# Two heads' scores and row maxima on one TensorE: the second head one product behind the first, and all eight PSUM banks in one ring

## What is computed

```python
q = (x @ Wq + bq).reshape(b, lq, H, D)
k = (embeds @ Wk + bk).reshape(b, lk, H, D)
v = (embeds @ Wv + bv).reshape(b, lk, H, D)
scores = jnp.einsum('bqhd,bkhd->bhqk', q, k) * SCALE
attn = jax.nn.softmax(scores, axis=-1)
ctx = jnp.einsum('bhqk,bkhd->bqhd', attn, v).reshape(b, lq, AD)
return ctx @ Wo + bo
```

## Time and profile before

| | us |
|---|---|
| median of three runs | 3068.25 |
| lowest and highest | 3066.65, 3070.2 |
| the profiled execution | 3069.01 |
| its span | 3067.2 |

### The profile page before, as it was taken

The page is one execution under the profiler, slowest core; times in us unless marked ns, Lnnn a source line. Parts: engine busy times, 40 slices in busy tenths (PEclk is TensorE's granted clock), DMA queues, the critical chain, the costliest instruction groups (busy, mean ns, idle before and its releaser), DMA issues.

```text
span 3067.2 us, 83608 instructions
## 1 busy us (share of the span) xinstructions
PE 2833.7 (92%) x28504; PEld 2329.2 (76%) x28504; DVE 2158.0 (70%) x4113; ACT 1687.2 (55%) x3422; POOL 2128.3 (69%) x1708
## 2 busy tenths in 40 slices
PE   5799999999999999999999999999999999998371
PEld 3688887888888888888888888888788888886241
DVE  6777777777777777777777777777777777774104
ACT  2466665656656656656566566566565665663020
POOL 2377777777777777777777777777777777776305
PEclk9799999999999999999999999999999999998586
DMA  3100000000000000000000000000000000000022
GB/s 97 40 1 12 2 13 3 13 2 12 3 2 13 2 13 2 13 3 13 2 13 3 2 13 2 13 2 13 3 13 2 14 14 2 2 1 1 21 92 62
DMA packets 65446, 42.02 MB, mean 14 GB/s; under 512 B 6614, under 2 KB 62635, under 8 KB 65010
## 3 DMA queue, kind: packets, MB, share of 16 engines
q1 hardware_dynamic: 62962, 32.35, 3.7%
q0 software_dynamic: 2048, 3.91, 0.5%
HBM read 28.15 MB, written 8.39 MB: 12 GB/s over the span
## 4 chain that ended last, share of the span: by engine, by line
PE 89%; issue 5%; POOL 3%; DVE 1%; ACT 0%; DMA 0%; POOLq 0%; DVEq 0%; ACTq 0%
PE ps L1315 28%; PE ps L1329 23%; PE ps L1289 8%; PE ps L1278 4%; PE ps L1279 3%; PE ps L1280 3%; PE ps L1262 3%; PE ps L1263 3%; PE ps L1264 3%; PE ps L1338 2%; PE ps L1347 2%; PE ps L1269 2%; PE ps L1437 1%; PE ps L1444 1%; PE ps L1297 1%
## 5 line engine op out<-in xcount | busy, mean ns | idle before, releaser
L587 POOL TENSOR_TENSOR key_sums<-key_sums,prob_T 128x512 f32<-128x512 f32 (+1 forms) x1408 | 1811.7, 1287 | 120.8 <-ACT prob_T L749 3.8
L977 DVE TENSOR_REDUCE mx<-ps 128x1 f32<-128x400 f32 (+1 forms) x2048 | 1077.0, 569 | 507.7 <-PE ps L1289 467.2
L749 ACT ACTIVATE prob_T<-ps 128x512 f32<-128x512 f32 x1536 | 834.1, 596 | 232.0 <-PE ps L1315 214.0
L1329 PE MATMUL ps<-prob_T,v_sb 128*64 128x256 f32 (+1 forms) x6656 | 742.4, 380 | 0.9 <-ACT prob_T L752 0.9
L1329 PEld LDWEIGHTS ps<-prob_T,v_sb 128*64 128x64 f32 (+1 forms) x6656 | 479.7, 137 | 242.1 <-issue 3.6
L583 POOL TENSOR_TENSOR key_sums<-prob_T 128x512 f32<-128x512 f32 x128 | 164.8, 1288 | 564.2 <-PE ps L1315 451.8
L1315 PE MATMUL ps<-shift,shift_w 64*128 64x256 f32 (+1 forms) x3328 | 509.5, 300 | 0.1
L1315 PE MATMUL ps<-q_hi,k_hi 64*128 64x256 f32 (+1 forms) x3328 | 476.6, 280 | 0.0
L1315 PE MATMUL ps<-q_lo,k_hi 64*128 64x256 f32 (+1 forms) x3328 | 475.1, 279 | 0.0
L1315 PE MATMUL ps<-q_hi,k_lo 64*128 64x256 f32 (+1 forms) x3328 | 473.7, 278 | 0.0
L738 ACT COPY heads_raw<-ps 128x256 f32<-128x256 f32 x128 | 47.7, 372 | 672.9 <-PE ps L1329 672.9
(11 more groups left out here) (173 smaller groups left out, 3600.0 us busy)
## 6 DMA issues: line engine op xcount, KB each, us to landing
ctx_raw<-in_ctx_dram SPq DMA_DIRECT2D x16, 768.0 KB
tables<-in_L_ffn_W_dram SPq DMA_DIRECT2D x16, 256.0 KB, 3.7
slots_in<-zeros SPq DMA_DIRECT2D x32, 64.0 KB
xs<-in_x_dram SPq DMA_DIRECT2D x8, 256.0 KB, 3.1
xres<-in_x_dram SPq DMA_DIRECT2D x8, 256.0 KB, 2.9
v_sb<-slots_in SPq DMA_DIRECT2D x8, 256.0 KB, 2.7
slots_out<-v_sb SPq DMA_DIRECT2D x8, 256.0 KB, 4.0
out_dram<-x1s SPq DMA_DIRECT2D x8, 256.0 KB, 2.4
```

Source lines behind the costliest of these rows:

```text
L587: op = nc.gpsimd.tensor_tensor(acc[0:rows, :, :], acc[0:rows, :, :], prob_T[0:rows, :, k, :], ALU.add)
L749: nc.scalar.activation(prob_T[:, h, 2 * i:2 * i + 2, :].rearrange("p k t -> p (k t)"), ps[:, bank, :], ACT.Exp).then_inc(ring_act, 1)
L977: v.tensor_reduce(mx[:, qt, h, c:c + 1], ps[:, at.bank("mx", r, c, qt, h), 0:WID[c]], AX.X, ALU.max).then_inc(ring_dve, 1)
L1329: last = mm(ps[h * DH:h * DH + DH, HEADS, 0:T], v_sb[0:rows, r % NJ // 2 % 2, k, v0 + h * DH:v0 + h * DH + DH], prob_T[0:rows, h, k, :], s ...
```

## The change

Three things are changed together.

1. The ring has all eight banks, and the result of `attend` is a place in it ("pv", the last of a slot). Its own semaphores go; `attend` waits for the bank of its place and for the last exponential.
2. A unit is issued in another order. Head 1's score products stand one step behind head 0's, and the two products of the maxima fill the holes: A0, M1, A1, B0, A2, B1, ... A7, B6, M0, B7. Each of the four banks is waited for on its own. The list of places has the order A, M1, B, M0, so with eight banks each of the four needs the bank that the same kind of product had in unit `i` - 2. The wait for B's bank stands ahead of A1, since `bank_of` for it is called right behind A0 and M1.
3. `ring_full` is no longer counted by scores and maxima: head 0's and head 1's have a counter each, `rows_full[h]`.

VectorE reduces head 1's maxima before head 0's in each pair. No product, exponential, reduction or copy is added or taken away.

```diff
-RING = (0, 1, 2, 3, 4, 5, 6)
-HEADS = 7
+RING = (0, 1, 2, 3, 4, 5, 6, 7)
...
         for i, unit in enumerate(MAX_UNITS):
+            if i < UNITS:
+                put("act", "s", s, i, 0)
             if following:
-                maximum(s + 1, unit)
+                maximum(s + 1, unit, 1)
             if i < UNITS:
-                for h in range(2):
-                    put("act", "s", s, i, h)
+                put("act", "s", s, i, 1)
+            if following:
+                maximum(s + 1, unit, 0)
...
+        put("act", "pv", s)
...
-                copy(heads_raw[:, :], ps[:, HEADS, 0:T]).then_inc(heads_free, 1)
+                act.wait_ge(ring_full, at.full("pv", r))
+                copy(heads_raw[:, :], ps[:, at.place_of("pv", r), 0:T]).then_inc(ring_act, 1)
...
-            def maximum(at, r, c, qt):
+            def maximum(at, r, c, qt, h):
                 pe.wait_ge(kh_ok, at.n(4, r, c + 1))
                 pe.wait_ge(qh_ok, at.n(1, r, 1))
-                banks = banks_of(at, *[("mx", r, c, qt, h) for h in range(2)])
...
+            def score_unit(at, s, i, unit):
+
                 tiles = [k for k in (2 * i, 2 * i + 1) if k < KT]
...
+                steps = [(n, k, step) for n, k in enumerate(tiles) for step in range(4)]
+
+                first, = banks_of(at, ("s", s, i, 0), also=[("k", s, 3), ("q", s), ("sh", s)] if i == 0 else [])
+                for at_step, part in enumerate(steps):
+                    ahead = score_step(s, 0, first, *part)
+                    if at_step == 0:
+                        if unit:
+                            maximum(at, s + 1, *unit, 1)
+                        second = bank_of(at, "s", s, i, 1)
+                    else:
+                        score_step(s, 1, second, *steps[at_step - 1])
+                ahead.then_inc(rows_full[0], 1)
+                if unit:
+                    maximum(at, s + 1, *unit, 0)
+                score_step(s, 1, second, *steps[-1]).then_inc(rows_full[1], 1)
...
             def attend(at, r):
-                wait(pe, heads_free, at.n(1, r, 0))
-
-                _, count = at.freed("s", r, UNITS - 1, 1)
-                pe.wait_ge(ring_act, count)
+
+                bank, = banks_of(at, ("pv", r), also=[("s", r, UNITS - 1, 1)])
```

More of the change, by code:

```diff
@@ L53, with maker @@
 UNITS = 7
+MAKERS = ("rows0", "rows1", "all")
+def maker(key):
+    return f"rows{key[-1]}" if key[0] in ("s", "mx") else "all"
 def value_fills(s):
@@ L65, in batch_fills, with maximum @@
     put = lambda owner, *key: fills.append((key, owner))
-    def maximum(r, unit):
-        for h in range(2):
-            put("dve", "mx", r, *unit, h)
+    def maximum(r, unit, h):
+        put("dve", "mx", r, *unit, h)
     if kind == "start":
@@ L79, in batch_fills @@
         for unit in MAX_UNITS:
-            maximum(0, unit)
+            maximum(0, unit, 1)
+            maximum(0, unit, 0)
         for c in range(4):
@@ L123, in owned @@
 def owned(kind, upto=None):
-    owners = [o for _, o in FILLS[kind][:upto]]
-    return {"full": len(owners), "act": owners.count("act"), "dve": owners.count("dve")}
+    fills = FILLS[kind][:upto]
+    owners, makers = [o for _, o in fills], [maker(key) for key, _ in fills]
+    return {"act": owners.count("act"), "dve": owners.count("dve"), **{m: makers.count(m) for m in MAKERS}}
 def bank_at(kind, place):
@@ L138, in __init__ @@
         self.start = {}
-        for of in ("full", "act", "dve"):
+        for of in ("act", "dve", *MAKERS):
             n_start, n_first, n_mid = (owned(k)[of] for k in ("start", "first", "mid"))
@@ L170, in full @@
     def full(self, *key):
-        return self._count("full", *self.find(*key))
+        return self._count(maker(key), *self.find(*key))
     def freed(self, *key):
@@ L179, in bank, with place_of @@
         return bank_at(self.kind, PLACE[self.kind][key])
+    def place_of(self, *key):
+        own, place = self.find(*key)
+        return bank_at(self._kind(own), place)
     def held_by(self, *key):
@@ L402, in decoder_layer @@
         ring_full = sem("ring_full")
+        rows_full = [sem(f"rows_full{h}") for h in range(2)]
         ring_act = sem("ring_act")
@@ L717, in values_out @@
                 if n == 0 and at.kind != "start":
-                    wait(act, pv_ok, at.n(1, 2 * g - 3, 1))
+                    if at.kind != "first" or g > 1:
+                        act.wait_ge(ring_full, at.full("pv", 2 * g - 3))
                 src = ps[:, at.bank("v", g, n), :].rearrange("p (k n) -> p k n", n=2 * P)
@@ L974, in maxima @@
                 for c, qt in units:
-                    for h in range(2):
-                        dve.wait_ge(ring_full, at.full("mx", r, c, qt, h))
+                    for h in (1, 0):
+                        dve.wait_ge(rows_full[h], at.full("mx", r, c, qt, h))
                         v.tensor_reduce(mx[:, qt, h, c:c + 1], ps[:, at.bank("mx", r, c, qt, h), 0:WID[c]],
@@ L1298, in row_shift @@
                 last.then_inc(ring_full, 1)
-            def score_unit(at, s, i):
-                banks = banks_of(at, *[("s", s, i, h) for h in range(2)],
-                                 also=[("k", s, 3), ("q", s), ("sh", s)] if i == 0 else [])
-                tiles = [k for k in (2 * i, 2 * i + 1) if k < KT]
-                rows = P if i < UNITS - 1 else KREM
-                for n, k in enumerate(tiles):
-                    cols = slice(k * P, k * P + rows)
-                    for step in range(4):
-                        for h in range(2):
-                            lanes = slice(h * DH, h * DH + DH)
-                            keys_part = (shift_w[lanes, 0:rows], k_hi[s % 2][lanes, cols], k_hi[s % 2][lanes, cols],
-                                         k_lo[s % 2][lanes, cols])[step]
-                            query_part = (shift, q_hi[s % 2], q_lo[s % 2], q_hi[s % 2])[step]
-                            last = mm(ps[0:rows, banks[h], n * T:n * T + T], keys_part, query_part[lanes, :],
-                                      start=(step == 0), stop=(step == 3))
-                            if step == 3 and k == tiles[-1]:
-                                last.then_inc(ring_full, 1)
@@ new lines, in score_step @@
+            def score_step(s, h, bank, n, k, step):
+                rows = P if k < KT - 1 else KREM
+                lanes, cols = slice(h * DH, h * DH + DH), slice(k * P, k * P + rows)
+                keys_part = (shift_w[lanes, 0:rows], k_hi[s % 2][lanes, cols], k_hi[s % 2][lanes, cols],
+                             k_lo[s % 2][lanes, cols])[step]
+                query_part = (shift, q_hi[s % 2], q_lo[s % 2], q_hi[s % 2])[step]
+                return mm(ps[0:rows, bank, n * T:n * T + T], keys_part, query_part[lanes, :],
+                          start=(step == 0), stop=(step == 3))
@@ L1390, in _ @@
             for unit in MAX_UNITS:
-                maximum(at, 0, *unit)
+                maximum(at, 0, *unit, 1)
+                maximum(at, 0, *unit, 0)
             for c in range(4):
```

33 lines of the change are left out of this document (15 added, 18 removed).

## The result

| | kernel before | changed kernel |
|---|---|---|
| median, same chip (7 runs each) | 3067.44 us | 3055.71 us |
| lowest and highest | 3064.69, 3070.2 | 3054.17, 3060.12 |
| the profiled execution | 3069.01 | 3059.33 |
| its span | 3067.2 | 3057.5 |

The ratio is 0.9965 (95% interval 0.9953 to 0.9976): 12 us faster, where 72 were forecast, and outside the range of 2978 to 3046. The sign was right and the size was not.

A forecast was written before the change was run, and what follows sets the result against it. A TensorE-ScalarE-TensorE loop over two units, 2.46 us against 2.26 undisturbed, was taken as the bound. Saving 0.57 us in each of 126 slots gives 72 us: 3068.25 - 72 = 2996 us, range 2978 to 3046.

The forecast's parts named there:

- The old bound: In the score units, a TensorE-ScalarE-TensorE loop sets the pace: 2.46 us per two units, against 2.26 undisturbed.
- The wait for head 1's bank: In the units' new order, the loop through head 1's exponential shrinks to 2.26 to 2.27 us per two units.
- v0 at 8.06, a gain of 0.57 a slot: At a slot's first value product: it starts at 8.06 us instead of 8.63, gaining 0.57 us a slot.
- the 0.05 between exponential and product: At bank waits on the matmul itself, register step already done: the product starts 0.05 us after the exponential, not 0.13.
- So the gain is passed on whole: Behind v0, VectorE, row shift and GpSimd hold nothing up, so 126 slots x 0.57 give 72 us.
- Cost of the removed waits: At the semaphores and attend's bank: renamed semaphores and the waits for attend's banks cost nothing.
- Rival 1: In the units, unequal neighbouring products run in step: units of 1.19 us, gain 29 us, 3039 us; chance 0.17.
- Rival 2: On TensorE's sequencer, extra register steps and waits make it fall behind: 3034 to 3059 us; chance 0.10.
- the closing part: Signs in the new profile: units of 1.13 to 1.14 us if right; "issue" idle before L1306 or L1324 for Rival 2.
- Rival 3: In the score steps, the lag breaks loading ahead: steps of 0.17 instead of 0.12 us, 3324 us; chance 0.08.
- Rival 4: Behind v0, the row shift or denominators take the gain back: about 3066 us; chance 0.05.
- the 9 of the clock row: In TensorE's profile through the whole middle: read as full speed, 2.4 GHz, with nothing to gain.

The follow-up runs named there:

- gateB0_pad40: The changed kernel with 40 unused semaphore increments ahead of the loop and the wait for head 1's score bank moved from A1 to B0: 3000.09 us.
- lag7_pad37: The changed kernel's new unit order, but with the old ring of seven banks and attend's own bank, 37 increments for alignment: 3069.61 us, ratio 1.0008 to the kernel before.
- ring8_pad98: The ring of eight with attend's result in it, but the kernel before's unit order and single counter, 98 increments for alignment: 3016.57 us, ratio 0.9832.
- after_pad40: The changed kernel with 40 unused semaphore increments ahead of TensorE's loop, its head again 233 instructions ahead of a block edge: 3006.93 us, ratio 0.9804 to the kernel before.
- after_pad213: The changed kernel with 213 unused semaphore increments ahead of the loop, its head 60 instructions ahead of a block edge: 3033.66 us.
- after_v0first: The changed kernel with 40 increments for alignment and the first value products issued ahead of the last maxima pair: 3025.67 us, ratio 0.9854 to the kernel before.

## Why the prediction was wrong

Its steps in their order:

- **The old bound: right.** Loop of TensorE, ScalarE and TensorE over two units; the units stretched in the earlier trace rows are gone.
- **The wait for head 1's bank, 2.26 to 2.27 us for two units: right by a hair.** Units come at 1.13. gateB0_pad40 shows that this wait still took 0.02 to 0.03 us a slot.
- **What gets the credit: wrong.** The prediction works out the unit as the place of the gain and treats the lag and the ring as one. lag7_pad37 (3069.6) and ring8_pad98 (slot 8.61, as with both) show that the gain comes from when v0 can start, and that the ring of eight alone gives it.
- **v0 at 8.06, a gain of 0.57 a slot: the right mechanism, over-sized by 0.09; the term is the 0.05 between exponential and product.** Measured are 0.48. In the changed kernel v0 starts 0.13 us after its exponential ends, where 0.05 was taken from the earlier trace rows. ScalarE's timeline has the exponential that frees v0's bank (the last of two, together 1.08 us from 1083.80), TensorE's has v0:

```profile
1083.80 1.08 ACT L767 ACTIVATE prob_T<-ps 128x512 f32<-128x512 f32 x2
```

```profile
1084.45 0.63 PE L1306 MATMUL ps<-k_hi,q_hi 64*128 64x402 f32 x2
1085.01 0.39 PE L1297 MATMUL ps<-wv_hi,ctx_hi 128*128 128x256 f32 x1
```

  1083.80 + 1.08 = 1084.88, v0 at 1085.01. Line L1258 in the stretch from 1084.89 to 1085.00 shows what stands between them, a register step of TensorE's sequencer:

```profile
L1258 PEldq ALU_OP  x1: 32/32/32, 1084.9 to 1084.9; - x1
```

  In all 98 slots outside the jumps that have value products, such a step starts 0.06 us after the exponential's end and v0 0.06 to 0.07 after the step. In the kernel before no step stands there in any of them, and v0 comes 0.05 after the exponential. So v0 lost the form from which the 0.05 was read, the register step done beforehand, and has the 0.13 that the prediction itself reads for a wait ahead of a register step. Why the step is no longer done ahead is open. The last two maxima don't hold v0: the second starts 0.37 us before it, and in ring8_pad98 v0 follows its pair after 0.27. (The prediction calls this pair "ready before that"; its first product starts at 1084.45, 0.05 after the first of the two exponentials, whose bank it inherits.) 126 x 0.09 = 11 us, and after_pad40 (3006.9) is 11 above the forecast of 2996. A middle slot with four value banks lasts 20.2 us, where 20.1 was forecast.
- **"So the gain is passed on whole": the step that failed.** The sum took 126 equal slots and so put at nothing what the change does to the 13 that follow a jump. Work behind v0 did pass the gain on (VectorE, which reduces its maxima without a break up to 1086.5, GpSimd and the row shift hold nobody), but the change also moved the program. 52 us went into instruction fetch and the half clock behind it. 2996 + 11 + 52 = 3059, and 3055.7 were measured; 2 of the 3 us between are the shorter gaps ahead of these slots.
- **Cost of the removed waits: nought, the prediction said.** That is true of their time. But 40 fewer instructions ahead of the loop moved its head from 233 to 17 instructions ahead of a block's edge, and that is where the loss comes from: after_pad40 puts 40 increments in their place and takes 49 us less.
- **Rival 1, neighbours of unequal length in step: no.** Units are 1.13, not 1.19. **Rival 2, the sequencer falls behind: no**; no "issue" stands before L1306 or L1324 within a slot without a jump. But an "issue" before L1324 is what the closing part told the reader to look for, it is there behind the jumps, and the time fell inside this rival's span of 3034 to 3059: the right number for another reason, by luck. **Rival 3, the lag breaks the loading ahead: no**, a step is 0.11 to 0.12. **Rival 4, the wait only moves:** for the lag alone this is what happened, at v0 itself and not behind it.

The clue was there beforehand. The chain of the kernel before says "issue 5%", 150 us which the prediction never took apart, and the branch record of L1397 shows a branch of 3.6 us in each turn. The prediction also reads the 9 of the clock row as full speed. A 9 stands for 90% or more, and it hides that behind 5 of 13 jumps TensorE ran at the half clock already in the kernel before, as in this stretch:

```profile
641.90:645.30 3.40, 3.40 (x36) 3.40 (x34) 2.11 (x4) 2.09 (x4) 1.66 (x2) 0.50 0.00 0
```

The place of the loop head and its distance to an edge could be counted in both programs.

## What to carry to other kernels

When an edit adds or removes instructions ahead of a loop on a queue that is the bound, work out where the loop's head falls in the queue's blocks of 256 instructions; leave enough behind it in its block (here 100 were enough and 60 were not), with instructions that do nothing if need be, and time a change only between kernels that are equal in this. Read the slot right behind a jump by itself, for a mean over slots hides it. Where several banks are waited for in turn, ask which producer's bank each product inherits: one bank more in the ring can change the heir, and that was worth more than a new order of the products. Before a product is moved into a hole, count how often the new order changes between products on 64 and on 128 rows.

## What the runs showed of the hardware that was not expected

- A jump back on TensorE holds its queue for 3.4 to 4.1 us (means of 13), of which 1.6 to 2.4 remain visible behind 5.6 us of queued `attend` (the gap to the next slot, 1.9 to 2.7, less the 0.31 of other slots).
- Behind a jump the next block of instructions is usable 2.6 to 3.4 us after work resumes. A head 17 or 18 instructions ahead of the edge costs a gap of 2.0 to 2.8 us, 60 ahead up to 1.4, 100 ahead none.
- A gap of 2 us behind the jump was followed by the half clock for 3.4 to 6.8 us; the gap of 0.9 us in after_pad213 shown above was not. The 1.5 to 1.8 us gap of the jump itself is followed by it in 5 of 13 turns before the change and in 4 of after_pad40.
- Matmuls of 400 and of 256 columns in the two halves of the array, 0.04 to 0.07 us out of step, cost nothing.
- A change between products on 128 and on 64 rows cost 0.09 us one way and 0.20 + 0.11 the other, with all banks free (after_v0first).
- A semaphore increment costs up to 0.13 us of TensorE's time when 35 stand in a row behind `attend`, and about 0.04 when 18 do; five behind each `attend` cost nothing (the ninth slot starts at 299.8 us in after_pad40, at 299.7 in the changed kernel).
